# Cutting the second experts' tile tables in two, with early loads of full tiles, in a fused two-layer kernel

## What is computed

```python
x = x + attention0(layernorm(x))                 # 16 heads, causal
x = x + experts0(layernorm(x))                   # top 2 of 8 experts
x = x + linear_attention1(layernorm(x))          # per batch, no softmax
x = x + experts1(layernorm(x))                   # top 1 of 8 experts

# experts1, on n = 4096 rows:
probs = softmax(x_flat @ w_gate + b_gate)
route_p, route_idx = max(probs), argmax(probs)
h = relu(x_flat @ W1[e] + b1[e])                 # 128 -> 512
y = h @ W2[e] + b2[e]                            # 512 -> 128
out = y[route_idx] * route_p
```

## Time and profile before

| what | us |
|---|---|
| three runs | 665.36, 666.56, 669.21 |
| median | 666.56 |
| profiled execution | 669.52 |
| its span in the trace | 667.44 |
| granted clock, mean of the span | 0.893 |
| VectorE's tables, last start | 566.33 |
| last scatter of the routing program | 567.87 |
| first transposes of the second experts | 575.35 |
| transposes of pair 19 | 651.56 |

### The profile page before, as it was taken

One profiled execution on the slowest core, in us unless ns is written; L12 is line 12 of the kernel. 1 busy time (PEld: TensorE's weight loads), 2 busy tenths in 40 slices (PEclk: granted clock), 3 DMA queues, 4 the chain that ended last, 5 costly groups with the idle time before them and its releaser, 6 DMA issues. The chain is left out here.

```text
span 667.4 us, 15359 instructions
## 1 busy us (share of the span) xinstructions
PE 532.7 (80%) x4916; PEld 439.3 (66%) x4931; DVE 449.2 (67%) x1287; ACT 354.0 (53%) x894; POOL 342.5 (51%) x459
## 2 busy tenths in 40 slices
PE   3189999999899998865989999999167561499996
PEld 2146666666666665643889989999155450498995
DVE  6476777878998797673777755553379877365662
ACT  2014457555655565443557656665347674265653
POOL 2003334434376536665746777776441547054555
PEclk9557999999999999987899999999567885699999
DMA  6563444445455445144423332221590125323330
GB/s 167 104 147 63 101 110 110 103 102 102 97 121 123 107 94 121 39 163 170 94 57 82 97 93 81 80 75 48 154 364 20 66 71 164 84 82 88 92 101 19
DMA packets 59525, 69.37 MB, mean 104 GB/s; under 512 B 9241, under 2 KB 50657, under 8 KB 57148
## 3 DMA queue, kind: packets, MB, share of 16 engines
q1 hardware_dynamic: 51168, 52.48, 31.6%
q0 software_dynamic: 7168, 14.77, 6.8%
q10 hardware_dynamic: 1116, 1.22, 0.9%
HBM read 45.31 MB, written 23.67 MB: 103 GB/s over the span
## 5 line engine op out<-in xcount | busy, mean ns | idle before, releaser
L616 DVE TENSOR_REDUCE mx<-max_ps 128x2 f32<-128x512 f32 (+1 forms) x192 | 128.4, 688 | 53.3 <-PE max_ps L277 51.4
L457 ACT ACTIVATE pT<-sc_ps 128x1536 f32<-128x1536 f32 x64 | 92.8, 1451 | 79.0 <-PE sc_ps L305 75.4
L1189 POOL DMA_INDIRECT expert_rows<-yt,go x72 | 78.7, 1093 | 28.6 <-issue 19.8
L1367 ACT ACTIVATE hT<-h_ps,wb 128x128 f32<-128x128 f32 x288 | 78.3, 386 | 20.2 <-PE h_ps L1414 20.2
L862 POOL TENSOR_TENSOR turn<-eps 128x1 f32<-128x1 f32 x64 | 12.6, 198 | 145.4 <-ACT pT L457 145.3
L58 POOL DMA_INDIRECT expert_queues<-rxr,rseats x64 | 65.7, 1026 | 26.8 <-issue 17.4
L1255 DVE COPY wb<-wpack 128x1156 f32 x72 | 53.6, 787 | 34.3 <-issue 26.9
L1414 PE MATMUL h_ps<-xT,wb 128*128 128x128 f32 x576 | 72.0, 279 | 0.5 <-ACT xT L1358 0.5
L274 PE MATMUL max_ps<-mask_qk,identb 128*128 128x256 bf16 (+1 forms) x177 | 57.5, 325 | 18.0 <-DMA wpack<-parts_scratch 13.9
L1532 POOL DMA_INDIRECT out_x<-yt,go x40 | 44.5, 1113 | 52.1 <-DVE go L1578 43.6
L1424 PE MATMUL y_ps<-wb,hT 128*128 128x128 f32 x576 | 70.0, 275 | 0.0
(11 more groups left out here) (307 smaller groups left out, 1113.1 us busy)
## 6 DMA issues: line engine op xcount, KB each, us to landing
wpack<-in_wpack SPq DMA_DIRECT2D x2, 4112.0 KB, 15.5
parts_scratch<-parts SPq DMA_DIRECT2D x16, 384.0 KB, 3.6
xt<-expert_queues SPq DMA_DIRECT2D x40, 129.0 KB, 2.1
xt<-expert_queues SPq DMA_DIRECT2D x72, 64.5 KB, 2.0
wpack<-parts_scratch SPq DMA_DIRECT2D x24, 192.0 KB
kst<-parts_scratch SPq DMA_DIRECT2D x24, 192.0 KB
qst<-parts_scratch SPq DMA_DIRECT2D x72, 64.0 KB
wpack<-parts_scratch SPq DMA_DIRECT2D x63, 64.0 KB
```

The costliest lines, as they stand in the source:

```text
L457: nc.scalar.activation(pT[u][:], sc_ps[:].rearrange("p a s -> p (a s)"), ACT.Exp, scale=float(DH) ** -0.5).then_inc(probs_ready, 1)
L616: nc.vector.reduce_max(mx[:, s, h0:h0 + n], max_ps[:, (k + 1) % 2, :].rearrange("p (h k) -> p h k", h=n), axis=AX.X).then_inc(unit_reduced, 1)
L1189: nc.gpsimd.indirect_dma_start(out=ys, out_offset=bass.IndirectOffsetOnAxis(ap=go[i % RING][:, s:s + 1].bitcast(mybir.dt.uint32), axis=0), ...
L1367: last = nc.scalar.activation(hT[i % 2][:, s, c, :], h_ps[i % 2][:, s, c * RT:(c + 1) * RT], ACT.Relu, bias=wb[i % 4][:, s, FF + c:FF + c ...
```

## The change

The second experts' 40 tiles are taken in two parts (SECOND): the first 8 pairs, 16 whole tiles, from the counts of the first 24 token tiles; the other 12 pairs from the final counts. count_tiles, find_experts and find_rows get the list of phases as an argument. The first part runs in bodies 16 to 18 of bridge; the second in bodies 0 and 1 of the second experts. tables and its buffers go.

GpSimd issues 28 of the 32 scatters in bridge, the other four first of all in the second experts; the first 24 count on one semaphore, the last eight on another. Load 0 waits for the first 24 alone, load 8 for the rest, the tails and the second part of the tables.

The tails' row numbers are copied at bridge's end. All eight tails are stored by SyncE, two behind each of the loads 3 to 6. The second experts become straight code, with an explicit loop in Python, and the load's wait on go_ready goes (y_ready stays). In attention, mask_ready is merged into ident_ready.

```diff
-            pe.wait_ge(mask_ready, 1)
+            pe.wait_ge(ident_ready, 3)
...
+SECOND = ((0, 8), (8, 20))
+EARLY_TILES, SENT = 24, 28
...
-def count_tiles(nc, t, link, p):
+def count_tiles(nc, t, link, phases, p):
-    if p < len(PHASES) - 1:
+    if p < len(phases) - 1:
...
-    dve.wait_ge(t["tabled"], p + 1)
+    dve.wait_ge(t["tabled"], tabled + p + 1)
...
 def second_experts(nc, t, out):
         @block.gpsimd
+            for j in range(SENT, NT):
+                scatter_choice(nc, t, j)
+            for i in range(NI):
+                give(i)
...
         @block.sync
+            def load(i):
+                if i == SECOND[0][0]:
+                    sp.wait_ge(t["scattered1"], 16 * EARLY_TILES)
+                if i == SECOND[1][0]:
+                    sp.wait_ge(t["scattered_d"], 16 * (NT - EARLY_TILES))
+                    sp.wait_ge(t["tails_stored"], 16 * E * 2)
+                    sp.wait_ge(t["tabled"], len(PHASES) + 2)
+                rows = [sp.value_load(tidx[0:1, 1, i * 2 + s:i * 2 + s + 1], min_val=0, max_val=E * REGION - RT) for s in range(2)]
+                if i >= 4:
+                    sp.wait_ge(xT_done, i - 3)
+                    sp.wait_ge(y_ready, i - 3)
...
+            def store_tail(e):
+                row = sp.value_load(t["tails"][0:1, e:e + 1], min_val=0, max_val=E * REGION - RT)
+                sp.dma_start(queue[bass.ds(row, RT), :], t["nothing"][:, 0:W]).then_inc(t["tails_stored"], 16)
+
+            for i in range(NI):
+                load(i)
+                if 3 <= i < 7:
+                    store_tail(2 * i - 6)
+                    store_tail(2 * i - 5)
...
         @block.vector
+            copy_w(0)
+            copy_w(1)
+            for i in range(NI + 2):
+                if i >= 2:
+                    take_y(i - 2)
+                if 0 <= i - 1 < NI:
+                    take_go(i - 1)
+                if i + 2 < NI:
+                    copy_w(i + 2)
+                if i == 0:
+                    count_tiles(nc, t, link, SECOND, 1)
+                    find_experts(nc, t, link, SECOND, 1)
+                if i == 1:
+                    find_rows(nc, dve, t, link, SECOND, 1, len(PHASES))
...
+def scatter_choice(nc, t, j):
+    nc.gpsimd.indirect_dma_start(out=t["queue1"], out_offset=bass.IndirectOffsetOnAxis(ap=t["rseats"][:, 0, j:j + 1], axis=0),
+                                 in_=t["rxr"][:, j, :, :].rearrange("p k a -> p (k a)"),
+                                 in_offset=None).then_inc(t["scattered1" if j < EARLY_TILES else "scattered_d"], 16)
...
 def bridge(nc, t, dram, ys):
-            for j in range(NT):
+            for j in range(SENT):
                 scatter(j)
...
                 for g in choices(i):
                     choose(g)
-            tables(nc, dve, t, 1, bufs, link, counted)
+                if i == NSEQ:
+                    count_tiles(nc, t, link, SECOND, 0)
+                if i == NSEQ + 1:
+                    find_experts(nc, t, link, SECOND, 0)
+                if i == NSEQ + 2:
+                    find_rows(nc, dve, t, link, SECOND, 0, len(PHASES))
+            link(nc.vector.tensor_copy(t["tails"][:], filled[:]))
```

More of the change, by code:

```diff
@@ L988 @@
 NCST = E + NTHR + n_tiles(2) + E + E + 1
[L991 to L1026, removed]
@@ L1029, in table_buffers @@
[L1029 to L1041, removed]
@@ L1514, in has @@
[L1514 to L1520, removed]
+        y_stored = t["y_stored1"]
+        xT_done, xT_ready, w_ready, go_ready, biased = sem("xT_done"), sem("xT_ready"), sem("w_ready"), sem("go_ready"), sem("biased")
+        h_done, hT_ready, y_done, y_ready, step = sem("h_done"), sem("hT_ready"), sem("y_done"), sem("y_ready"), sem("step")
+        block = ctx.enter_context(nc.Block(no_gpsimd_drain=True))
@@ L1536, in body, with give @@
[L1536 to L1542, removed]
-                    pool.wait_ge(y_stored[par], 16 * NI)
+            last_place = pool.to_reg(NT * P - 1)
+            def give(i):
+                pool.wait_ge(go_ready, i + 1)
+                pool.wait_ge(y_ready, i + 1)
+                for s in range(2):
+                    nc.gpsimd.indirect_dma_start(out=out, out_offset=bass.IndirectOffsetOnAxis(ap=go[i % 4][:, s:s + 1].bitcast(mybir.dt.uint32), axis=0),
+                                                 in_=yt[i % 2][:, s, :], in_offset=None, bounds_check=last_place,
+                                                 oob_is_err=False).then_inc(y_stored[i % 2], 16)
@@ L1558, in _ @@
-            sp.wait_ge(t["scattered1"], 16 * NT)
-            sp.wait_ge(t["tails_stored"], 16 * E * (1 + w))
-            for i in range(3):
-                load(i, i)
-            def body(i, r):
-                if has(i + 3):
-                    load(i + 3, (r + 3) % 4)
-            run(sp, body)
+            def load(i):
[9 more added lines that the diff above has]
+                    sp.wait_ge(y_ready, i - 3)
+                for s in range(2):
+                    sp.dma_start(xt[i % 4][:, s, :], queue[bass.ds(rows[s], RT), :]).then_inc(xt_loaded[i % 4], 16)
@@ L1605, in _ @@
[L1605 to L1617 removed]
+                if i >= 2:
+                    dve.wait_ge(y_stored[i % 2], (i - i % 2) * 16)
@@ new lines, in take_y @@
+                nc.vector.tensor_tensor(yt[i % 2][:], y_ps[i % 2][:, 0:2 * RT].rearrange("p (s d) -> p s d", d=D), wb[i % 4][:, :, PK:PK + D],
+                                        ALU.add).then_inc(biased, 1)
+                dve.wait_ge(biased, i + 1)
+                for s in range(2):
+                    last = nc.vector.scalar_tensor_tensor(out=yt[i % 2][:, s, :], in0=yt[i % 2][:, s, :], scalar=xt[i % 4][:, s, W - 1:W],
+                                                          in1=xt[i % 4][:, s, D + 1:W - 1], op0=ALU.mult, op1=ALU.add)
@@ L1677, in second @@
                     for c in range(FC):
-                        last = nc.tensor.matmul(y_ps[par][:, s * D:(s + 1) * D], hT[par][:, s, c, :],
-                                                wb[r][:, s, FF + FC + c * D:FF + FC + (c + 1) * D], start=(c == 0), stop=(c == FC - 1))
+                        last = nc.tensor.matmul(y_ps[i % 2][:, s * D:(s + 1) * D], hT[i % 2][:, s, c, :],
+                                                wb[i % 4][:, s, FF + FC + c * D:FF + FC + (c + 1) * D], start=(c == 0), stop=(c == FC - 1))
                 last.then_inc(y_done, 1)
-            transpose_in(0, 0)
-            def body(i, r):
-                first = isinstance(i, int) and i == 0
-                if first:
-                    hidden(i, r)
-                if has(i + 1):
-                    transpose_in(i + 1, (r + 1) % 4)
-                if has(i) and not first:
-                    hidden(i, r)
-                if has(i - 1):
-                    second(i - 1, (r - 1) % 4)
-            run(pe, body)
+            transpose_in(0)
+            for i in range(NI + 1):
+                if i == 0:
+                    hidden(0)
+                if i + 1 < NI:
+                    transpose_in(i + 1)
+                if 0 < i < NI:
+                    hidden(i)
+                if 0 <= i - 1 < NI:
+                    second(i - 1)
 def wait_results(sp, t, slots, w):
@@ L2133, in program @@
         bridge(nc, t, dram, ys)
-        experts(nc, t, 1, 1, dram["out"])
+        second_experts(nc, t, dram["out"])
 def kernel(**inputs):
```

198 lines of the change are left out of this document (70 added, 128 removed).

## The result

The changed kernel measured 664.15 us (median) against 668.08 for the kernel before, beside each other: a ratio of 0.9926, interval 0.9909 to 0.9944. That is 4.9 us less, 3.7 to 6.1; 6.4 were forecast, just outside that interval. The medians alone stand 3.9 apart; one of the 15 executions of the changed kernel, 671.06, was in a slower state and is left out of the ratio. The profiled execution has a span of 661.8 against 667.4, but not all of the 5.6 belong to the change: in the two traces bridge (its first matmul) starts at 473.22 and 471.83, behind code whose instructions differ in the one merged semaphore of attention alone, and over all traces of these kernels on like chips that start lies between 467.7 and 474.5.

What follows compares the result with a forecast made beforehand. Bound by waits: the turn into the second experts, the ring of four xt buffers, the tail. 7.05 us earlier less 2.4, then 61.3 for 15 bodies with tails, gave 6.4 less: 660.2 from 666.56, range 656.0 to 664.5.

Steps and rivals of the forecast that it cites:

- The turn: Routing program to second experts: VectorE done at 563.55 against 566.51, first transposes at 568.3, 7.05 us earlier.
- The next step: VectorE's end to the second experts' first transposes: 4.74 us, taken from the turn between attention and first experts.
- rival 4: Block's end waits until GpSimd has drained, start not earlier; even so within 1 us of forecast start; no chance given.
- The second table part: On VectorE ahead of take_y(0) in the second experts: pair 4's transposes at 583.8, giving back 2.4 of 7.05 us.
- Two tails per load: On SyncE behind loads 3 to 6: 0.5 us lost in all, bounds nothing and 1.5.
- Unrolling: Straight code in the second experts: 4.05 us per body against 4.205, 60.75 for 15 bodies; bounds 58.5 and 63.1.
- The ring: Four xt buffers in the second experts: load(i) waits for y_ready of pair i-4, at 4.1 to 4.3 us.
- The clock: TensorE idle about 2.4 us before pair 4's transposes: granted clock stays at 1.00, priced at nothing.
- rival 3: Slower: the gap before pair 4's transposes drops the clock to 1.2 GHz; four cold bodies give 671.4; chance 0.10.
- The sum of 6.4: Second experts: pair 19's transposes at 645.1 against 651.56, 6.4 us earlier, same tail behind; median 660.2.
- rival 1: Gain mostly given back: routing program's table part 5.1, ring stays at 4.205; 3.6 us earlier, median 663.0; chance 0.20.

Runs made afterwards that it cites:

- the doubled table: Changed kernel with count_tiles and find_experts of the second part run twice in body 0 of the second experts; ratio 0.9994 on the longer chip.
- The moved tails: Changed kernel with four tails issued by ScalarE before its first copy, four by SyncE behind load 3; ratios 0.9936 (longer chip) and 0.9899.

## Why the prediction was right, and where it was off

**The turn.** Right. VectorE decided the block's end, and the scatters were no bound. The table part in bridge took 1.32 + 1.33 + 1.25 = 3.9 for the 4.0 that I took, and the tails' copy 0.14 for 0.4; the seats and gates around them took 4.5 for the 5.0 that I carried over, as two waits between them (0.26 and 0.17) are gone. Together VectorE was done 0.9 earlier than forecast. The next step was 0.5 too short: 5.25 from VectorE's end to T(0), where the earlier turn had 4.74; so T(0) came out nearer than either step, which is luck. That a drained GpSimd would have changed little (rival 4) was near the truth in size, but the run with 32 scatters says that the stream runs about three scatters ahead.

**The second table part.** Right in mechanism and size, and the doubled table shows it: take_y(0) began at 577.32, 11.4 behind T(0), where the sum had 11.5. T(4) was 15.78 behind T(0) for the forecast 15.5, and the doubled table moved it by 4.04.

**Two tails per load.** Mis-sized. The step said 0.5 with an upper bound of 1.5, on the ground that bodies of 3.8 and 4.2 in turn take up part of it. The moved tails show 1.4 to 2.1 up to T(8) (16.8 against 18.2 and 18.9). I had priced a load with two tails at 4.4 on SyncE's queue; it took 4.65 twice and 5.20 once. And the slack that I counted on was not there: y_ready(1) came at 581.75 and y_ready(2) at 586.84, their loads at 583.30 and 587.93, so 1.5 and 1.1 late, and TensorE had nothing in hand against it.

**Unrolling.** The step that failed. It gave 2.3 us (63.08 to 60.75 for 15 bodies) to straight code, and the runs give it nothing: ratios of 1.0003 and 1.0031, and 0.4 less in this stage. 4.05 per body was taken and 4.12 measured behind T(8) (45.35 / 11), with 4.15 before. Long and short bodies did take turns, as I said, but they had done so in the loop too (4.63, 3.92, 4.32 and 3.89 from T(8) on in the trace before); what lifted the old mean to 4.205 were the two long bodies in a row ahead of T(6) and T(7), 4.75 and 4.92:

```profile
592.32 0.38 PE L1656 MATMUL xT_ps<-ident,xt 128*128 128x128 f32 x2
597.07 0.43 PE L1656 MATMUL xT_ps<-ident,xt 128*128 128x128 f32 x2 [0.76 <-DMA xt<-expert_queues]
601.99 0.43 PE L1656 MATMUL xT_ps<-ident,xt 128*128 128x128 f32 x2 [0.86 <-DMA xt<-expert_queues]
605.88 0.38 PE L1656 MATMUL xT_ps<-ident,xt 128*128 128x128 f32 x2
```

The ring itself I took at 4.1 to 4.3, near the one pair of rows that I had read, and it goes up to 4.7. The chain of waits of the changed kernel shows the landings of later loads (start, us, what):

```profile
606.43 2.66 DMA xt<-expert_queues
...
615.00 2.04 DMA xt<-expert_queues
...
622.95 2.33 DMA xt<-expert_queues
```

The bodies that end with these waits took 4.72, 4.10 and 4.39; the free ones between them 3.85. The difference lies in how long a load takes to land, and not in the loop.

**The clock.** Right to price it at nothing. The stretches of the changed kernel:

```profile
568.00:570.00 2.00, 2.00 (x12) 2.00 (x12) 1.76 (x8) 0.00 (x0) 0.00 (x0) 0.52 0.61 132
570.00:572.00 2.00, 1.45 (x14) 1.24 (x13) 1.54 (x6) 1.28 (x5) 0.00 (x0) 1.00 0.53 161
...
577.00:581.00 4.00, 2.01 (x19) 1.82 (x17) 3.19 (x9) 1.63 (x7) 1.50 (x2) 1.00 0.27 72
```

It rose about 4 behind T(0), as in the earlier trace rows, and stayed at 1.00 over the 2.70 of idle. The gap of 6.82 in the doubled table did bring the half rate. The Trainium skill (TensorE: Matmul & The Clock Gate, "Why this matters for your kernels") warns of long idle gaps between bursts of matmuls, not of any gap, and both traces agree with it; my prediction read it too widely when it applied it to a gap of some 2.4. Even 6.82 would not have made rival 3 true: one body was cold and took 2.1 more than the 3.8 of a warm one, where rival 3 needed 2.3 bodies at 2.8 more each to use up the gain.

**The whole.** The sum of 6.4 was 1.5 too high by the ratio and 2.7 by the two traces, where the terms are 2.1 between T(4) and T(8), of which the tails are some 1.5, and 0.8 behind T(8), less 0.1 before T(4); the 0.6 and the 0.8 that are not the tails are the unrolling. The measured 664.15 lies only 0.35 inside the range's upper end of 664.5, beside a median before of 668.08 and not the 666.56 that I had subtracted from. That it lies inside is owed to the range, which took in most of rival 1, more than to the sum. Rival 1 (3.6 us) was as near as the forecast; of its two reasons the ring at 4.2 was near the truth, and the table part at 5.1 was not (3.9). The ring, for which I had no rival, was worth most: with load(i) tied to y_ready(i-4), part of any earlier start is handed back, and two more buffers give most of that back and 0.33 per body (4.12 to 3.79).

## What to carry to other kernels

Before moving work ahead, look at what the ring behind it is tied to: a load that waits for the last reader's engine, here VectorE, passes every delay of that engine on to TensorE, while two more buffers cost 4 KB per partition (two of 2 x 258 floats) and took 5 us off the old kernel and 8 off the changed one. Price register reads on a queue as you price transfers: two tail stores of 1.1 us each behind each of three loads cost 1.4 to 2.1 us in their stage, and stores of a single row in their place cost as much. Before crediting a gain to unrolling, look in the trace for what the limiting engine waits for: here TensorE waited for loads, and writing the loop out gave nothing.

## What the runs showed of the hardware

- With 32 scatters ahead of the barrier, VectorE got past it 1.9 us later than with 28, at about 562.6, though the record of the last scatter began only at 566.48. So, by that estimate, GpSimd's instruction stream passed the barrier about 3.9 us, three records, before its last indirect DMA's record began.
- After 2.70 of idle TensorE's granted clock was still 1.00; after 6.82 it was 0.50, the next body took 5.92 in place of 3.8, and the one behind it was warm again.
- A load of two tiles with its two register reads took 2.24 us of SyncE's queue and a store with one read 1.06; one load and two stores took 4.63 to 5.20, and 4.85 to 4.90 where the stores moved one row for 128.
- Seven traces of changed kernels, all with the same code up to bridge, start it between 467.67 and 473.55: 5.9 us apart, more than the change itself is worth. A gain read off two spans needs a point of reference inside them.
